# Score columns of the middle attention units: by way of DRAM rows and broadcast DMA in place of TensorE transposes

## The reference

```python
# layer 0, graph attention (layer 3 is the same with one head of 256)
Wh = (X @ W).reshape(B, N, H, F)
e_src = jnp.einsum('bnhf,hf->bnh', Wh, a_src)
e_dst = jnp.einsum('bjhf,hf->bjh', Wh, a_dst)
e = jax.nn.leaky_relu(e_src[:, :, None, :] + e_dst[:, None, :, :], LRELU_ALPHA)
e = jnp.where(mask, e, NEG_INF)
alpha = jax.nn.softmax(e, axis=2)
Hout = jax.nn.elu(jnp.einsum('bijh,bjhf->bihf', alpha, Wh))
# layer 1, three turns: aggregate over the edges, then a GRU cell
m = jnp.einsum('bnd,de->bne', h, weight[i])
aggr = jnp.einsum('bst,bsd->btd', A, m)
h = _gru_cell(aggr, h, w_ih, w_hh, b_ih, b_hh)
```

## Time and profile before

| | |
|---|---|
| median of 3 runs | 2705.61 us (2705.57 to 2707.29) |
| the profiled execution: its own time | 2710.0 us |
| its span, first to last instruction | 2708.2 us |
| PE busy | 2652.5 us, 98% of the span |
| DVE, ACT, POOL busy | 77%, 61%, 50% |
| mean share of the 16 DMA engines | under a tenth after the first 150 us |
| mean granted TensorE clock | 0.990 of full speed |

### The profile page before, as it was taken

How to read it: one execution, slowest core, us unless ns; L and a number is a source line. 1 busy time by engine, 2 the same in 40 slices (tenths; PEclk the granted TensorE clock), 3 DMA queues, 4 the chain that set the end, 5 groups by cost and what they waited for, 6 DMA issues and landing times.

```text
span 2708.2 us, 49251 instructions
## 1 busy us (share of the span) xinstructions
PE 2652.5 (98%) x15793; PEld 2307.3 (85%) x15793; DVE 2097.5 (77%) x5196; ACT 1642.3 (61%) x4217; POOL 1352.5 (50%) x1361
## 2 busy tenths in 40 slices
PE   7999999999999999999999999999999999999995
PEld 6988888888888888888888888888888888888884
DVE  7877777777787777787777787777788777788765
ACT  5556565666565666565666565666565666565553
POOL 1345555445555445555445555455555455555452
PEclk9999999999999999999999999999999999999997
DMA  5300000000000000000000000000000000000000
GB/s 154 88 19 25 22 19 25 27 23 28 23 19 24 27 23 29 23 19 25 26 23 28 23 19 25 27 23 27 24 19 24 27 23 27 24 19 23 11 9 24
DMA packets 109966, 75.33 MB, mean 28 GB/s; under 512 B 7024, under 2 KB 109552, under 8 KB 109680
## 3 DMA queue, kind: packets, MB, share of 16 engines
q1 hardware_dynamic: 89984, 54.28, 6.9%
q10 hardware_dynamic: 19696, 17.44, 1.9%
HBM read 54.93 MB, written 16.78 MB: 26 GB/s over the span
## 4 chain that ended last, share of the span: by engine, by line
PE 92%; DVE 1%; issue 1%; ACT 1%; POOL 0%; DVEq 0%; POOLq 0%; ACTq 0%
PE psum L870 57%; PE psum L724 10%; PE psum L783 6%; PE psum L858 3%; PE psum L907 3%; PE psum L857 3%; PE psum L763 2%; PE psum L772 2%; PE psum L741 2%; PE psum L800 1%; PE psum L844 1%; PE psum L799 1%; PE psum L791 1%; DVE stats L1259 0%; ACT x L1099 0%
## 5 line engine op out<-in xcount | busy, mean ns | idle before, releaser
L1484 POOL TENSOR_TENSOR ht<-ht,g_n 128x512 f32<-128x512 f32 (+1 forms) x198 | 272.3, 1375 | 466.9 <-ACT g_n L1087 464.5
L870 PE MATMUL psum<-ag_h,wc_h 128*128 128x512 f32 (+1 forms) x1188 | 487.0, 410 | 0.2 <-DVE ag_l L1343 0.2
L870 PE MATMUL psum<-ht_h,whh_h 128*128 128x512 f32 (+1 forms) x1188 | 482.6, 406 | 1.3 <-ACT g_z L1082 1.3
L870 PE MATMUL psum<-ht_l,whh_h 128*128 128x512 f32 (+1 forms) x1188 | 461.9, 389 | 0.0
L870 PE MATMUL psum<-ht_h,whh_l 128*128 128x512 f32 (+1 forms) x1188 | 461.7, 389 | 0.0
L870 PE MATMUL psum<-ag_l,wc_h 128*128 128x512 f32 (+1 forms) x1188 | 461.5, 388 | 0.0
L870 PE MATMUL psum<-ag_h,wc_l 128*128 128x512 f32 (+1 forms) x1188 | 461.5, 388 | 0.0
L1427 POOL TENSOR_SCALAR rstd<-moments 128x2 f32<-128x2 f32 x256 | 100.6, 393 | 446.7 <-DVE moments L1263 443.7
L870 PEld LDWEIGHTS psum<-ht_h,whh_l 128*128 128x128 f32 x1188 | 224.0, 189 | 50.2
L870 PEld LDWEIGHTS psum<-ag_h,wc_l 128*128 128x128 f32 x1188 | 223.6, 188 | 49.8
L1078 ACT ACTIVATE g_r<-psum,bias_rz 128x512 f32<-128x512 f32 (+1 forms) x198 | 133.5, 674 | 216.0 <-PE psum L870 215.8
(11 more groups left out here) (153 smaller groups left out, 7020.9 us busy)
## 6 DMA issues: line engine op xcount, KB each, us to landing
adj_i<-in_adj_dram SPq DMA_DIRECT2D x128, 128.0 KB, 2.2
x_in<-in_x_dram SPq DMA_DIRECT2D x64, 256.0 KB, 2.9
out_dram<-out_t ACTq DMA_DIRECT2D x64, 256.0 KB, 2.1
part<-in_adj_dram SPq DMA_DIRECT2D x32, 256.0 KB, 3.2
adj_g<-in_adj_dram SPq DMA_DIRECT2D x31, 256.0 KB, 3.9
ih_raw<-in_L_gnn_w_ih_dram SPq DMA_DIRECT2D x1, 768.0 KB, 9.3
hh_raw<-in_L_gnn_w_hh_dram SPq DMA_DIRECT2D x1, 768.0 KB, 10.6
wl_raw<-in_L_gnn_weight_dram SPq DMA_DIRECT2D x1, 768.0 KB, 9.8
```

Of the source, the lines that this page charges most:

```text
L870: last = mm(dst, s, m, start=(first and k == 0), stop=(last_part and k == len(flat) - 1))
L1484: tt(ht[k % 2][:, c, nodes_of(k)], ht[k % 2][:, c, nodes_of(k)], g_n[:, nodes_of(k)], ALU.subtract).then_inc(s_d, 1)
```

## The change

For the middle units (`pre` units 6 to 63 and `post` units 0 to 58) PE has no share in the scores any more. There are two new steps, both on SP's queue. `att_rows` waits until ACT has copied both graphs' `wh`, and stores the destination score columns to a small DRAM tensor as rows, one DMA for each graph. Every number is an element of its own: 128 numbers for each head and graph. `att_spread` waits for both stores and loads the row back with a broadcast, so that each of the 128 partitions receives the whole row in `scores`. For `pre` that is one DMA of 256 KB for each graph, for `post` one DMA of 128 KB for the unit. ACT's share of `att_scores` then adds the bias in place, from `scores` to `scores`, and waits for the DMA and not for PE. What `att_scores` was is now named `att_direct`, and is used for the units of the start and the end.

```diff
+            def att_rows(kind, u):
+                L, n = LAY[kind], rowed(kind, u)
+                w = slot("wh", "att_wh", kind, u, 0)
+                sp.wait_ge(L.wh_ready, 2 * u + 2)
+                for spread in L.spread:
+                    after(sp, spread, 16 * (n - 1))
+                with nc.allow_non_contiguous_dma(reason="a score column becomes a row"):
+                    for q in range(2):
+                        sp.dma_start(L.kept[n % 2][q].rearrange("h n -> n h"), wh[w][:, q, D + L.heads:D + 2 * L.heads]).then_inc(L.rows_kept, 16)
+
+            def att_spread(kind, u, q):
+
+                L, i = LAY[kind], rowed(kind, u) % 2
+                ti = take(sp, kind + "_t", "att_spread", kind, u, q)
+                sp.wait_ge(L.rows_kept, 32 * (rowed(kind, u) + 1))
+                n = L.heads if kind == "pre" else 2
+                kept = L.kept[i][q:q + 1].rearrange("a h n -> a (h n)") if kind == "pre" else L.kept[i].rearrange("q h n -> h (q n)")
+                sp.dma_start(L.scores[ti][:, 0:n, :].rearrange("p h n -> p (h n)"), kept.broadcast_to([P, n * P])).then_inc(L.spread[q], 16)
...
+            def att_scores(kind, u, q):
+
+                L = LAY[kind]
+                w = slot("wh", "att_wh", kind, u, 0)
+                ti = slot(kind + "_t", "att_spread", kind, u, q)
+                act.wait_ge(L.spread[q], 16 * (rowed(kind, u) + 1))
+                cells = [(q, h) for h in range(L.heads)] if kind == "pre" else [(0, 0), (1, 0)]
+                for k, (g, h) in enumerate(cells):
+                    f(L.scores[ti][:, k, :], L.scores[ti][:, k, :], ACT.Identity, bias=wh[w][:, g, D + h:D + h + 1]).then_inc(L.shifted, 1)
```

All three order tables are written anew. Of `HALF` the lines around the end and the start of a half show the kind of change:

```diff
-gru_hn(-1,2,0)  att_scores(pre,1,1,1)  pre_load(2,0)  gru_load(1)
...
+gru_hn(-1,2,0)  att_pv(post,-2,0)  rel_rest(-2,1)  gru_new(0,0,1)  att_exp(post,-2,0)  att_norm(pre,1,0)
+        att_spread(pre,1,1,1)  att_scores(pre,1,1,0)  att_scores(pre,1,1,1)  att_res(post,-2,0)
...
+gru_z(0,1,1)  post_load(-1,1)  att_rows(pre,2,0)  rel_h1(-1,0)  gru_norm(-1,1)
```

More of the change, by code:

```diff
@@ L75 @@
 HALF = """
-rel_h1(-2,0)
-gru_z(-1,1,1)
-gru_in(-1,1,1)  rel_split(-2,1)  rel_adjt(-2,1)  rel_y1(-2,0)  rel_rest(-2,0)
+gru_in(-1,1,1)  rel_split(-2,1)  rel_adjt(-2,1)  rel_y1(-2,0)  att_spread(pre,1,0,0)  att_spread(pre,1,0,1)  rel_rest(-2,0)
 gru_agg(0,0,0)
-gru_agg(0,0,1)  att_scores(pre,1,0,0)  att_scores(pre,1,0,1)  att_store(post,-3,0)
-gru_hn(0,0,0)  rel_norm(-2,0)  gru_new(-1,1,0)  rel_mask(-2,1)
-gru_rzh(0,0,0)  att_prob(pre,1,0)  att_xt(post,-2,0)
-gru_r(0,0,0)  gru_n(-1,1,1)  att_pt(pre,1,0,0)
@@ L84 @@
-gru_z(0,0,0)
-gru_in(0,0,0)  att_pt(pre,1,0,1)  pre_load(1,1)  gru_new(-1,1,1)
-gru_hn(0,0,1)  gru_split(-1,1)  att_wh(post,-2,0,0)  att_wh(post,-2,0,1)  rel_h1(-2,1)  att_pv(pre,1,0)  gru_turn(-1,1,0)
-        gru_turn(-1,1,1)  gru_n(0,0,0)  att_xt(pre,1,1)  att_exp(pre,1,0)  att_res(pre,1,0)
-gru_rzh(0,0,1)  att_scores(post,-2,0,0)  att_wh(pre,1,1,0)
-gru_r(0,0,1)  rel_y1(-2,1)
-gru_z(0,0,1)  rel_rest(-2,1)  att_prob(post,-2,0)  att_wh(pre,1,1,1)  gru_new(0,0,0)
-gru_in(0,0,1)
-gru_agg(-1,2,0)  att_scores(pre,1,1,0)  att_norm(post,-3,1)  att_pt(post,-2,0,0)  gru_n(0,0,1)
@@ L231 @@
+gru_in(-1,1,1)  gru_new(-1,1,0)  rel_h1(-3)  att_pt(post,-4,0)  gru_n(-1,1,1)  rel_split(-2)  rel_y1(-3)  rel_rest(-3)
+        gru_new(-1,1,1)  rel_adjt(-2)  att_pv(post,-4)  gru_split(-1,1)  gru_turn(-1,1,0)  rel_norm(-3)  att_norm(post,-5)
 gru_agg(-1,2,0)
-gru_agg(-1,2,1)  rel_mask(-2)
-gru_hn(-1,2,0)  att_norm(post,-5)  att_store(post,-5)  att_wh(post,-3,0)  att_exp(post,-4)  att_wh(post,-3,1)
-        att_res(post,-4)
-gru_rzh(-1,2,0)
+gru_agg(-1,2,1)  att_store(post,-5)
+gru_hn(-1,2,0)  att_xt(post,-3)  rel_mask(-2)  rel_h1(-2)
@@ L823, in rel_rest @@
                 if u == 0:
-                    pe.wait_ge(s_wrs, 16)
+                    pe.wait_ge(s_rest, 48)
                 with pe.If(any_other > 0):
```

330 lines of the change are left out of this document (178 added, 152 removed).

## The result

The changed kernel takes 3126.61 us (median of 4 runs, 3120.51 to 3131.45), the kernel before 2705.59 us (4 runs beside it, 2704.57 to 2707.29). The ratio is 1.1547, 95% interval 1.1533 to 1.1561: slower by 421 us, where 64.6 us faster was forecast. The forecast was faster, and so was its whole range.

The account below looks back on a forecast made before the run. PE, never idle in the middle, was taken as the bound: 582 transposes at 0.111 us take 64.6 us off 2705.6, giving 2641.0 us, with added hops, moved loads and ends at zero. Range 2628 to 2675 us.

Parts of the forecast that it names:

- The step that failed: SP's single-number stores in the middle: 22 ns a number, adding 1.4 us (pre) or 0.4 us (post) to 2.1 us landing.
- the lower end: Store price per number: 22 ns from below, chosen over 0.15 to 0.21 us because middle DMA engines are busy at 8%.
- the estimate by its access time: Skill page's 0.2 us HBM access per number: 64 numbers 12.8 us, chain about 6 us over budget, some 2820 us.
- The chain and its budget: Middle units: pre stores plus spreading load take 7.4 us, within 12.5 us covered by PE's queue, so cost nothing.
- The rival "slow stores": Middle pre units: 0.21 us a number, chain 17.2 us, 4.7 us over budget, 136 us in all, 2777 us; chance 0.06.
- The third rival: Middle halves: a 1.9 us PE wait each, then a lowered clock, costing 3.7 against 2.2 gained; 2749 us; chance 0.04.
- What is removed: PE's middle score transposes: 582 go at 0.111 us each, 64.6 us off the time.
- What is moved: pre_load and post_load behind SP's stores and spreading loads, and the new start and end: costed at nothing.
- 12 us for the ends: New start and end: worth zero, with some 12 us either way, a third of the idle time there.
- ACT reading from SBUF: ACT's middle score instructions: same number, reading SBUF instead of PSUM, perhaps a few per cent slower, with ACT not full.
- The spreading loads: SP's broadcast loads: 2.9 us for 256 KB (pre), 2.2 us for 128 KB (post), hidden behind PE's queue.
- What the text named as signs of being wrong: PE idle before att_pt or gate products, stores landing after 8 us, middle clock under full, or ends idle over 66 us.

Follow-up runs that it names:

- e5: Changed kernel with each single number stored 512 bytes apart in DRAM, stores still awaited, spreading loads reading input x: 2670.04 us.
- e14: Changed kernel with pre numbers stored as dense 16-byte elements, post numbers 64 bytes apart, spreading loads reading x: 2670.47 us.
- e6: Changed kernel with 128 partitions storing 512 contiguous bytes each in place of single numbers, spreading loads reading x: 2670.88 us.
- e10: Changed kernel with the single numbers stored 64 bytes apart in DRAM, spreading loads reading x: 2670.30 us.
- e2: Changed kernel without stores or spreading loads; ACT reads the wh column with a step of zero, no transposes for middle scores: 2669.30 us.
- e3: Changed kernel without the stores; spreading loads issued once wh is ready, reading input x: 2669.89 us.
- e1: Kernel before with the changed kernel's order of steps, scores by TensorE transposes throughout: 2723.95 us, ratio 1.0060.
- e13: Changed kernel with single numbers gathered in an SBUF row, copied whole to DRAM, then spread; computes the reference for this input: 2685.36 us.
- e4: As e3, but all stores are issued too, awaited only by the next user of their buffer: 3229.56 us.
- e8: As e4, but ACT's queue issues the stores and SP's the loads: 2745.90 us, ratio 1.0143.

## Why the prediction was wrong, point by point

**The step that failed** is the time of the stores: "I take the lower end, since the middle of the run has DMA engines busy at 8%". The two stores of a `pre` unit were put at 0.5 + 2.1 + 1.4 = 4.0 us and take 9.2 to 11.7 us in SP's row; those of a `post` unit, at 0.5 + 2.1 + 0.4 = 3.0 us, take 8.2. The step looked for the price of a single number, between 22 ns and 0.21 us, and multiplied it by the numbers per DMA engine. That was the wrong kind of price. Where the numbers stand apart, the same packets land after 1.5 us (`post`) and 1.9 us (`pre`, where the lower end gave 2.1 + 1.4 = 3.5 us). Where they are dense, a `post` store lands after 7.5 us, and SP's mean wait is 7.7 us for 256 numbers and 9.8 us for 1024, and not four times as long. Neither load of the earlier trace rows could show that, since a load writes nothing to DRAM.

**What the page had.** The Trainium skill, DMA: Bandwidth & Descriptors, in Specifications, warns of read-modify-write below 512 bytes. The sign came out as it warned, and the estimate by its access time (2820 us) lies within 10% of the result, but that is luck: it charged 0.2 us for each number, and by e5 a number has no such price. The runs differ from the warning in where the price lies: lone 4-byte stores (e5) and dense 16-byte ones (e14) are about as fast as 512-byte ones (e6), 1.9, 1.7 and 1.6 us to the landing of a `pre` store. Here the measurement decides. The same page, in Anatomy of one DMA, which tells it of DMAs that GpSimd issues, says that the final descriptor waits for the data write to have completed, with a long delay above all where the target is HBM. The quiet 5.5 us between the last packet and the landing agree, for DMAs that SP issues. That writes to one line queue up in the memory would fit all of this, but no run shows the mechanism itself.

**The chain and its budget** held where the stores are fast. With stores apart the chain of a `pre` unit is 2.4 + 0.8 + 4.4 (spreading load as in e10) = 7.6 us against the forecast 7.4, no wait of PE for the scores appears, and the time is that of e2, without any DMA of scores. In the changed kernel it is 9.2 to 11.7 + 0.8 to 2.6 + 4.1 = 14.1 to 18.4 us against a budget of 12.5.

**The rival "slow stores"** had the place and the sign, and was 350 us too small (2777). Its price, 0.21 us a number, was of the same wrong kind: by it the `post` units, with 16 numbers for each DMA engine, would not have overrun. It counted one overrun of 4.7 us in each half. In fact the `post` units run over too, the loads behind the stores come later, and the clock falls. The sum over the middle, against e3_spread_only's 2270.63 us of PE for 13229 matmuls in 2282 us:

- idle time of PE: 294 us against some 11 us, +283 us;
- the same 12992 matmuls would be busy 12992 × 2270.63 / 13229 = 2230.0 us at full clock and are busy 2387.8, +158 us. This fits the clock of 0.94: some 320 us at half speed do the work of 160.

Together 441 of the 457 us; the rest lies at the ends. The third rival had the clock's part of this (each wait gives some of it back a second time at the lower level), but with a short wait in mind: 44 us in all. It had the waits at 1.9 us a half, and they were about 10.

**What is removed**: forecast 64.6 us, measured 54.7 (e1 to e2). 0.111 us between starts is what a transpose takes in the chain; 94 ns is what came off with it. The 10 us of difference were not taken apart.

**What is moved** was costed at nothing, with 12 us for the ends. Part of that is the same failed step: "nothing but its pen and `adj_f` work is held up" had the loads some 4 us later, and behind the slow stores POOL waits 314.1 and 242.4 us for them. The order by itself cost 16 us, and most of it not at the ends but as half a microsecond in every half (e1). About half of that is a new wait for DVE before the products with `h_l`, 8.3 us in 28 waits in e1_order; it stays when the transposes are gone, here in e2_no_dma from 218 to 2500 us:

```profile
PE psum L762 <- DVE h_l L1349: 11.1, 28, 0.7
```

These two make the floor, 2669.3 us, 28 us worse than the forecast; the range (2628 to 2675) would just have held the kernel if the stores had been as assumed.

**ACT reading from SBUF** costs nothing that counts, as said: 390 ns an instruction against 375 from PSUM. **The spreading loads** too, as said (e3).

**What the text named as signs of being wrong** came: PE idle before `att_pt` and gate products released by ACT, a clock under full in the middle, SP waiting 9.8 us for the stores of a `pre` unit (the `post` stores land at 7.5 us, just under the 8 that it named).

## What to carry to other kernels

Before a column is turned into a row by DMA, ask where neighbouring numbers land in DRAM and not only how many descriptors there are: dense 4-byte writes to DRAM cost 6 us and more a transfer, and delay the completion of what is issued around them, on another queue too, even when nobody waits for them; the same numbers 64 bytes apart, or in elements of 16 bytes, cost nothing extra here, and written into SBUF next to nothing (4.6 us over the whole kernel). If a dense row in DRAM is needed, put it together in SBUF, in a buffer of its own, and copy it as a whole (e13). And where no row of a trace shows an operation, a price per element taken from another kind of transfer is no bound: a cheap kernel that has only this operation, or leaves only this out, is worth more than the sum.

## What the runs showed of the hardware that was not expected

- Stores of single numbers to DRAM, dense: 7.5 us to landing for 0.5 KB, with no packet in the record for the last 5.5 us of it. Eight bytes apart 3.1 us, 16 bytes and more 1.5 us. Stores of four times as many numbers (2 KB): 4.1 us at 8 bytes, 3.5 at 16, 2.0 at 64.
- Loads issued behind such stores land after 11.6 us in place of 3.9 to 4.4 (e4 and e3), and `adj_g`, on another queue than the stores, after 12.0 in place of 2.9 (e8 and e3).
- 256 KB read from one SBUF partition by 128 reads of 2 KB land after 16.0 us; out of one 2 KB row of DRAM after 3.6 to 4.5 us.
- ACT with a step of 16 bytes in input and output takes 517 to 528 ns for 128 columns in place of 390 to 393, DVE's masked minimum 397 ns in place of 292, PE's transposes 285 in place of 273.
